# Attention row maxima in 16 bits, subtracted by a product whose stationary operand is one column read with step zero

## The reference

```python
def _arsinh_norm(x, w, b):
    return w * jnp.arcsinh(x) + b
...
nb_k = kk[:, ri, ci].reshape(B, H, W, k * k, num_heads, hd)
nb_v = v[:, ri, ci].reshape(B, H, W, k * k, num_heads, hd)
scores = jnp.einsum('bijnd,bijmnd->bijnm', q, nb_k)
attn = jax.nn.softmax(scores, axis=-1)
out = jnp.einsum('bijnm,bijmnd->bijnd', attn, nb_v).reshape(B, H, W, C)
...
h1 = _arsinh_norm(h, n1_w, n1_b)
h = h + _na2d(h1, qkv_w, qkv_b, proj_w, proj_b)
h2 = _arsinh_norm(h, n2_w, n2_b)
ff = jax.nn.gelu(h2 @ mlp_w1 + mlp_b1, approximate=False) @ mlp_w2 + mlp_b2
return h + ff
```

## Time and profile before

| what | value |
|---|---|
| median of 3 runs | 4412.26 us (4411.27 to 4412.83) |
| profiled execution, span from first to last instruction | 4410.1 us |
| PE busy | 4291.9 us, 97% of the span |
| DVE busy | 3769.7 us, 85% |
| ACT busy | 3660.2 us, 83% |
| POOL busy | 3450.6 us, 78% |
| mean granted TensorE clock | 0.992 |

### The profile page before, as it was taken

How to read it: one execution, slowest core, us unless ns; L and a number is a source line. 1 busy time by engine, 2 the same in 40 slices (tenths; PEclk the granted TensorE clock), 3 DMA queues, 4 the chain that set the end, 5 groups by cost and what they waited for, 6 DMA issues and landing times.

```text
span 4410.1 us, 136683 instructions
## 1 busy us (share of the span) xinstructions
PE 4291.9 (97%) x53320; PEld 3082.4 (70%) x53320; DVE 3769.7 (85%) x7715; ACT 3660.2 (83%) x5377; POOL 3450.6 (78%) x4092
## 2 busy tenths in 40 slices
PE   5999999999999999999999999999999999999997
PEld 3677777767777777776777777777777767777775
DVE  5888888888888888888888888888888888888884
ACT  4888888888888888888888888888888888888884
POOL 2787887888788788888878878887887888788775
PEclk8999999999999999999999999999999999999998
DMA  4555555555555555555555555555555555555551
GB/s 118 130 137 144 136 139 139 141 140 138 140 140 137 143 136 139 139 139 140 138 144 135 138 141 139 140 138 142 136 138 139 140 139 139 141 139 137 140 134 51
DMA packets 593555, 600.06 MB, mean 136 GB/s; under 512 B 76558, under 2 KB 540560, under 8 KB 590352
## 3 DMA queue, kind: packets, MB, share of 16 engines
q1 hardware_dynamic: 592912, 591.32, 51.4%
HBM read 197.69 MB, written 135.40 MB: 76 GB/s over the span
## 4 chain that ended last, share of the span: by engine, by line
DVE 42%; PE 34%; issue 12%; POOL 11%; SPq 1%; ACT 1%; DMA 0%; POOLq 0%; DVEq 0%; ACTq 0%
PE ps L382 32%; DVE ln_u L777 8%; DVE ln_u L773 8%; POOL a_lo L1162 6%; DVE o_norm L882 6%; DVE ps L851 5%; POOL a_hi L1160 3%; DVE q_nat L818 2%; DVE y L845 2%; DVE recip L873 2%; DVE v_nat L832 2%; PE ps L406 2%; DVE o_lo L838 2%; DVE ln_u L770 1%; DVE maxima L857 1%
## 5 line engine op out<-in xcount | busy, mean ns | idle before, releaser
L1154 POOL TENSOR_TENSOR p_lo<-prob,p_hi 100x512 f16<-100x512 f32 x1024 | 1256.7, 1232 | 639.1 <-ACT p_hi L1072 639.1
L1071 ACT ACTIVATE prob<-ps 100x512 f32<-100x512 f32 x1024 | 613.6, 599 | 143.2 <-PE ps L382 141.8
L882 DVE TENSOR_TENSOR o_norm<-ps,recip 64x128 f32<-64x128 f32 x2048 | 591.3, 289 | 49.4
L1180 POOL TENSOR_TENSOR g_lo<-g,g_hi 128x512 f16<-128x512 f32 x512 | 595.9, 1164 | 41.0
L1072 ACT ACTIVATE p_hi<-ps 100x512 f16<-100x512 f32 x1024 | 617.2, 603 | 0.0
L382 PEld LDWEIGHTS ps<-v_win,p_hi 100*128 100x128 f16 x8192 | 484.7, 98 | 185.3 <-issue 15.3
L851 DVE TENSOR_REDUCE ps<-ps 128x8 f32<-128x800 f32 x512 | 509.5, 995 | 88.9 <-PE ps L382 84.8
L382 PE MATMUL ps<-w_hi,g_hi 128*128 128x256 f16 x2048 | 560.3, 274 | 0.0
L382 PE MATMUL ps<-w_lo,g_hi 128*128 128x256 f16 x2048 | 560.2, 274 | 0.0
L382 PE MATMUL ps<-w_hi,g_lo 128*128 128x256 f16 x2048 | 560.1, 273 | 0.0
L382 PE MATMUL ps<-v_win,p_hi 100*128 100x65 f16 x8192 | 516.5, 194 | 26.0 <-POOL p_lo L1154 15.8
(11 more groups left out here) (103 smaller groups left out, 11981.0 us busy)
## 6 DMA issues: line engine op xcount, KB each, us to landing
keys<-k_win SPq DMA_DIRECT2D x1536, 100.0 KB, 2.2
v_win<-v_rows SPq DMA_DIRECT2D x1024, 101.6 KB
queries<-q_nat SPq DMA_DIRECT2D x1536, 64.0 KB
v_rows<-v_nat SPq DMA_DIRECT2D x256, 260.0 KB, 5.6
xin<-in_x_dram SPq DMA_DIRECT2D x128, 512.0 KB, 4.5
out_dram<-y SPq DMA_DIRECT2D x256, 256.0 KB, 3.1
queries<-in_query_mask_dram SPq DMA_DIRECT2D x128, 160.0 KB
keys<-in_mlp_w_dram SPq DMA_DIRECT2D x2, 512.0 KB, 7.5
```

Of the source, the lines that this page charges most:

```text
L882: s = v.tensor_tensor(o_norm[r, c], av[r, :, HD * e:HD * e + HD], recip[c % 2][r].to_broadcast([NQ, PAIRS, HD]), ALU.mult)
L1071: act.activation(prob[b][0:NK], ps[0:NK, B_ST + b, :], ACT.Exp, scale=INV * INV).then_inc(prob_ready, 1)
L1154: pool.tensor_tensor(p_lo[b][0:NK], prob[b][0:NK], p_hi[b][0:NK], ALU.subtract).then_inc(p_lo_ready, 1)
L1180: pool.tensor_tensor(g_lo[:, m, :], g32[:, m, :], g_hi[:, m, :], ALU.subtract).then_inc(g_lo_ready, 1)
```

## The change

The row maxima are written once, by the reduction itself, as 16-bit numbers in SBUF: `maxima` shrinks to 128 x 2 x 4. `maximum_high`, `maximum_low`, `maxima_to_rows` and `max_rows` are gone, and with them `max_row`, three semaphores, four clears and one load at the start. `subtract_max` still has 8 products per slot of the same shape. The stationary operand is now one column of `maxima`, read 128 times with step zero (every one of the 128 output rows gets the same weights), and the moving one is minus the identity. So element (key, query) receives minus the maximum of that query. All partitions of the output are written with it, where the 28 rows past the 100 keys got zero before; they are not read. The maximum is subtracted as rounded to 16 bits.

```diff
@@ sync: the loads at the start
-                (ident16[:], ident16_c.bitcast(BF16)),
-                (key_max[:].rearrange("p a k -> p (a k)"), key_max_c.bitcast(BF16)),
+                (minus_ident[:], minus_ident_c.bitcast(BF16)),
@@ tensor
             def scores(t, par, k):
-                pe.wait_ge(maxrow_ready, signals(t, SLOTS, k))
+                pe.wait_ge(max_ready, signals(t, SLOTS, k))
...
-            def max_rows(t, k):
-                pe.wait_ge(max_ready, signals(t, SLOTS, k + 1))
-                pe.transpose(ps[:, B_S, MAXT_COLS].bitcast(BF16), maxima[k % 2][:], ident16[:]).then_inc(pe_max, 1)
...
             def subtract_max(t, c):
                 k = c // 2
                 if c % 2 == 0:
-                    pe.wait_ge(maxrow_ready, signals(t, SLOTS, k + 1))
+                    pe.wait_ge(max_ready, signals(t, SLOTS, k + 1))
                 for p in range(PAIRS):
-                    s = mm(ps[:, B_ST + c % 2, p * P:(p + 1) * P], key_max[:, (c % 2) * PAIRS + p, :], max_row[k % 2][:],
-                           stop=True)
+                    a = maxima[k % 2][:, c % 2, p:p + 1]
+                    column = bass.AP(a.tensor, a.offset, [list(a.ap[0]), [0, P]])
+                    s = mm(ps[:, B_ST + c % 2, p * P:(p + 1) * P], column, minus_ident[:], stop=True)
                 s.then_inc(pe_st, 1)
...
-                    max_rows(0, 0)
...
-                    if more:
-                        max_rows(ahead[0], ahead[2])
@@ vector
             def maximum(t, k):
                 v.wait_ge(pe_s, signals(t, SLOTS, k + 1))
-                v.tensor_reduce(maxima_of_pair(),
+                v.tensor_reduce(maxima[k % 2][:].rearrange("p n a -> p (n a)"),
                                 ps[:, B_S:B_S + 2, 0:PAIRS * NK].rearrange("p n (a k) -> p n a k", k=NK),
-                                AX.X, ALU.max).then_inc(max32_ready, 1)
-            def maximum_high(t, k):
...
-            def maximum_low(t, k):
...
-            def maxima_to_rows(t, k):
...
+                                AX.X, ALU.max).then_inc(max_ready, 1)
@@ vector, step: the calls of the three are gone
                     if more:
                         maximum(ta, ka)
-                        maximum_high(ta, ka)
-                        maximum_low(ta, ka)
...
-                    if more:
-                        maxima_to_rows(ta, ka)
```

More of the change, by code:

```diff
@@ L40 @@
 INV = 1.0 / WS
-M0 = 32
 MASK0 = 3 * HD
@@ L49 @@
 XT = 4
-N_LOADS = 13 + 2 * PAIRS
-N_ZERO = 11
+N_LOADS = 12 + 2 * PAIRS
+N_ZERO = 7
 V_BV, V_ALL = 8, 23
@@ L58 @@
 SETUP_QK, SETUP_V, SETUP_1, SETUP_P = 3, 4, 6, 7
-MAXT_COLS = slice(PAIRS * NK, PAIRS * NK + P // 2)
-MAX_COLS = slice(PAIRS * NK + P // 2, PAIRS * NK + P // 2 + HEADS)
 TURN_BANK = [1, 0]
@@ L83, in constants @@
         marks[WIN + r, :, r] = MASKED_K
[L85 to L88, removed]
     query = np.zeros((BPI, 2 * WIN, HEADS, TILES, TS, TS), np.float16)
@@ L104, in constants @@
         "ident": ident,
-        "ident16": bfloat16_bits(np.eye(P)),
+        "minus_ident": bfloat16_bits(-np.eye(P)),
         "key_marks": marks.reshape(2 * WIN, NK),
-        "key_max": bfloat16_bits(key_max.reshape(P, 2 * PAIRS * P)),
         "query_mask": query.reshape(BPI, 2 * WIN, HEADS * TILES * NQ),
@@ L112, in build @@
 def build(nc, x, qkv_w, qkv_b, proj_w, proj_b, n1_w, n1_b, n2_w, n2_b, mlp_w1, mlp_b1, mlp_w2, mlp_b2,
-          ident_c, ident16_c, key_marks_c, key_max_c, query_mask_c, out):
+          ident_c, minus_ident_c, key_marks_c, query_mask_c, out):
     x_rows = x.rearrange("i r j c -> (i r j) c")
@@ L128, in build @@
         ident = sb("ident", [P, P], F32)
-        ident16 = sb("ident16", [P, P], BF16)
-        key_max = sb("key_max", [P, 2 * PAIRS, P], BF16)
+        minus_ident = sb("minus_ident", [P, P], BF16)
         wqkv_hi, wqkv_lo = sb("wqkv_hi", [P, G, 3 * C], F16), sb("wqkv_lo", [P, G, 3 * C], F16)
@@ L158, in build @@
         p_lo = [sb(f"p_lo{i}", [P, 512], F16) for i in range(2)]
-        maxima = [sb(f"maxima{i}", [P, P], BF16) for i in range(2)]
-        max_row = [sb(f"max_row{i}", [P, P], BF16) for i in range(2)]
+        maxima = [sb(f"maxima{i}", [P, 2, PAIRS], BF16) for i in range(2)]
         recip = [sb(f"recip{i}", [P, PAIRS, 1], F32) for i in range(2)]
@@ L200, in build @@
             sem("pe_" + s) for s in ("x", "q", "k", "v", "proj", "m1", "m2"))
-        pe_s, pe_max, pe_st, pe_av, pe_ot = (sem("pe_" + s) for s in ("s", "max", "st", "av", "ot"))
+        pe_s, pe_st, pe_av, pe_ot = (sem("pe_" + s) for s in ("s", "st", "av", "ot"))
         xT_ready, h_ready, abs1, abs2, sum1, sum2 = (sem("dve_" + s) for s in ("xT", "h", "abs1", "abs2", "sum1", "sum2"))
@@ L205, in build @@
         q_lo_ready, k_lo_ready, v_lo_ready, o_lo_ready = (sem("dve_" + s) for s in ("q_lo", "k_lo", "v_lo", "o_lo"))
-        max32_ready, max_hi_ready, max_ready, maxrow_ready = (
-            sem("dve_" + s) for s in ("max32", "max_hi", "max", "maxrow"))
+        max_ready = sem("dve_max")
         recip_ready, norm_ready = sem("dve_recip"), sem("dve_norm")
@@ L227, in rows_of @@
             return ap.rearrange("p (i j) -> p i j", j=SIDE)
-        def maxima_of_pair():
-            return ps[:, B_S, MAX_COLS]
         def turned(o, half):
@@ L850, in maximum @@
                 v.wait_ge(pe_s, signals(t, SLOTS, k + 1))
-                v.tensor_reduce(maxima_of_pair(),
+                v.tensor_reduce(maxima[k % 2][:].rearrange("p n a -> p (n a)"),
                                 ps[:, B_S:B_S + 2, 0:PAIRS * NK].rearrange("p n (a k) -> p n a k", k=NK),
-                                AX.X, ALU.max).then_inc(max32_ready, 1)
-            def maximum_high(t, k):
-                v.wait_ge(max32_ready, signals(t, SLOTS, k + 1))
-                v.tensor_copy(maxima[k % 2][:, M0:M0 + HEADS], maxima_of_pair()).then_inc(max_hi_ready, 1)
-            def maximum_low(t, k):
[L860 to L863, removed]
-            def maxima_to_rows(t, k):
-                v.wait_ge(pe_max, signals(t, SLOTS, k + 1))
-                r = slice(M0, M0 + 2 * HEADS)
-                v.tensor_copy(max_row[k % 2][r, :], ps[r, B_S, MAXT_COLS].bitcast(BF16)).then_inc(maxrow_ready, 1)
+                                AX.X, ALU.max).then_inc(max_ready, 1)
             def sum_reciprocal(t, c):
@@ L912, in opening @@
                     maximum(0, 0)
-                    maximum_high(0, 0)
-                    maximum_low(0, 0)
-                    maxima_to_rows(0, 0)
             def step(t, u):
@@ L979, in _ @@
                 zero(t_[:].rearrange("p n g c q -> p (n g c q)").bitcast(U32), 0)
-            for t_ in (*maxima, *max_row):
-                zero(t_[:])
             for t in range(-3, 0):
```

## The result

The changed kernel takes 4353.6 us (median, 4353.1 to 4354.0) against 4411.8 of the kernel before on the same chip: a ratio of 0.9866, with a 95% interval of 0.9853 to 0.9879. That is 58 us less. The forecast was 4328 us, 84 us less, inside a range of 4294 to 4400: the sign held, and about 26 of the 84 us did not come.

What follows compares the result with a forecast made beforehand. PE was taken as the bound, with a nearly tight VectorE and GpSimd chain behind its small stalls. Terms of 30.7 + 24 + 29 = 84 us took 4412 to 4328 us, range 4294 to 4400.

Steps and rivals of the forecast that it cites:

- The bound: Whole band of 33.49 us: PE bounds all but some 0.6 us, which belong to a chain through VectorE and GpSimd.
- The subtracting products: PE, eight products per slot with a step-zero stationary operand: same 98 ns loads and 56 ns apiece, no gain or loss.
- The transposes, 30.7 us: PE: 512 removed transposes, four in a band, 0.060 us each on PE's own path, 30.7 us in all.
- Up to L406, 0.25 us: VectorE without the copy starts q_low 0.25 us earlier; 0.06 already counted, so 0.19 us x 125 bands = 24 us.
- From L406 to `a_lo`, 0.35 us: VectorE and GpSimd, slots 2 and 3: 0.35 us a band, 0.12 counted with the transposes, so 0.23 x 125 = 29 us.
- The limit that the prediction set for `sum1_`: VectorE, slot 2: ScalarE's root, ending at 2148.07, lets sum1_ start only 0.24 of a possible 0.53 us earlier.
- `p_lo` stays ahead of `sign1`: End of slot 3: GpSimd's p_lo, 0.24 us earlier, is still first; sign1 ends 1.1 us after it as before.
- The slow load: Step-zero weight loads in subtract_max lose the quick load: hidden in part 4398 us, chance 0.07; in full 4508 us, chance 0.11.
- Only the transposes' time comes: Rival: ScalarE's root, p_lo or b_lo takes up what VectorE gives, so the chain keeps its length; 4381 us, chance 0.20.
- That the two exclude each other: VectorE with two SBUF inputs and GpSimd seem to run one after the other: sign1 1.78 us against 1.22; changes no term.

Runs made afterwards that it cites:

- e6: Changed kernel with dense minus identity as stationary operand of the subtracting products instead of the step-zero maxima column, maxima not subtracted: 4354.2 us.
- e1: Changed kernel with a transpose of a 16-bit identity put back on PE alone, four per band, read by nothing: 4361.8 us.
- e5: Changed kernel with all three small VectorE instructions (rounding, remainder, copy) put back in slots 2 and 3: 4405.4 us.
- e2: Changed kernel with the VectorE copy from PSUM put back in slot 1 alone, between normalise and q_low: 4369.3 us.
- e9: Changed kernel with one exchange on VectorE in slot 1, v_low(t+2, 0) moved ahead of sum2_(t-1): 4323.9 us.
- e3: Changed kernel with the two small VectorE instructions (rounding, remainder) put back behind the reduction in slot 3 alone: 4361.6 us.
- e8: Changed kernel with GpSimd's p_lo of a band's last tile cut to 64 of its 512 columns: 4361.4 us.
- e10: Changed kernel with v_low moved ahead of sum2_ in slot 1, and the a_hi casts moved from GpSimd to VectorE behind the normalisation of slot 3: 4323.5 us.

## Why the prediction was right and wrong

*The bound.* Right: PE with two small stalls, and a chain through VectorE and GpSimd with hardly any slack. A band of 33.49 us became one of 33.02 in the changed kernel and of 32.79 with the exchange; the forecast was 32.83.

*The subtracting products.* Right, and shown: 98 ns per load, the same pace, and e6 equal.

*The transposes, 30.7 us.* The price of one (0.06) is right. That all four lie on the path is not: putting them back in the changed kernel costs 8 us (e1), and e5, which is without them, gains only 7 us on the kernel before.

*Up to L406, 0.25 us.* Right for this stretch: 12.54 to 12.23 us with the transposes in it, and e2 shows the copy's part by itself. Wrong as a term of the sum: in e2 the copy is worth 16 us and not 24, and in e5 the shorter stretch brings next to nothing, since `g_lo` doesn't come earlier with L390. The two stretches of the band were added up as if they were independent.

*From L406 to `a_lo`, 0.35 us.* This is the step that failed; it brought 0.15. The prediction let the 0.28 us of the two small instructions pass from slot 2 to `sum1_`. They were in fact 0.41, and they didn't pass: `sum2_` gave back 0.42. I had looked only at the instructions that the change removes and at what stands behind them, and not at those that it brings nearer to GpSimd's. PE's gain ahead of L406 (0.31 from the first product, and 0.12 less of the stall for `a_lo`) moved `sum2_` into the last 0.55 us of `g_lo`, where before it was the last 0.13. That the loss equals the saving, so that `sign2` starts at +5.8 in both kernels, is chance.

The limit that the prediction set for `sum1_` was the wrong one too. It let the root, whose end it put at 2148.07, decide, with 0.24 us to gain. `sum1_` starts at +9.41 in the changed kernel and also in e9, where it visibly waits for the root: the root lets it go 0.10 us after its end, and so gives only 0.15. But the start isn't what counts. `sum1_` ends about 1.08 us after `b_lo`, at +11.35 before and in the changed kernel and at +11.11 in e9, and `b_lo` hangs on `sign2` through GpSimd's `p_lo`.

The claim that `p_lo` stays ahead of `sign1` was wrong as well, by 0.02 us; by e3 that was worth 0.06 to 0.1 us, in favour of the changed order.

With the collision at `sum2_` out of the way (e9), the number comes out: `a_hi` 0.40 earlier for 0.35 forecast, 4324 us for 4328. The way there is in part luck. `p_lo` comes 0.24 earlier (+14.71 for +14.95), as forecast, but through `b_lo` and not through the root, and the other 0.16 is the order of `sign1` and `p_lo`, which the prediction had the other way round.

*The rivals.* The slow load is refuted by e6. "Only the transposes' time comes" has its grain: it named GpSimd and VectorE getting in each other's way as the reason, and this is what took the 26 us. It gave 4381; the changed kernel lies halfway between this and the forecast.

*That the two exclude each other.* In the kernel before, the changed one and e1 to e8, `sum2_` is due at +1.30 and `g_lo` ends anywhere from +1.44 to +2.13. In all ten the end of `sum2_` lies 1.08 us behind the end of `g_lo` (medians over some 100 bands each), so it does its work after `g_lo` and not beside it. In e9, where only 0.06 us of `g_lo` is left, it takes 1.21. The Trainium skill (SBUF — State Buffer, section SBUF: two separate sides) states this as a port pair shared by VectorE, when it has two SBUF inputs, and GpSimd, under an exclusive lock for the whole instruction; the durations named here agree with it.

What stays open: no run measures such a pair by itself, outside this kernel. The rest of the wait at L390 (22.9 us in the changed kernel, 23.0 in e9) was not tried.

## What to carry to other kernels

Where two engines exclude each other on some instructions, a removed instruction need not shorten a chain by its own time: write down the start and end of each exclusive pair and ask which pair the shift brings together. A busy time that grows on an engine with an unchanged list is the sign of it. When the time saved shows up nowhere, look for the instruction that became longer, in the next band too, and give the engine something else to do in that gap; here one exchanged pair of lines was worth 30 us in the changed kernel and nothing in the other. And measure from more than one zero: counted from L390 it looked as if `g_lo` came late, counted from the turn it had not moved.

## What the hardware showed that I had not expected

Less work on GpSimd (e8) made the kernel 8 us slower, and 1.2 us less per band (e10) changed nothing. A stationary operand read 128 times from one 16-bit element per partition loads in the same 98 ns as a dense one (e6). And two instructions that come due 0.02 us apart decided which of them took 1.2 and which 2.2 us, the same way throughout: in the changed kernel the last `p_lo` of a band takes 2.20 us in the median, and 2.20 to 2.21 from the tenth to the ninetieth percentile of the bands.
